# Three graph-attention layers and a relation layer on one core: layer 1's edge weights as a minimum with the mask

## The reference, cut to what matters

```python
def _L1_gnn_ref(x, adj, W, a):
    h = jnp.einsum('bnf,fo->bno', x, W)
    s1 = h @ a1
    s2 = h @ a2
    e = jax.nn.leaky_relu(s1[:, :, None] + s2[:, None, :], negative_slope=0.2)
    att = jnp.where(adj > 0, e, jnp.float32(NEG_BIG))
    att = jax.nn.softmax(att, axis=1)
    h_prime = jnp.einsum('bij,bjo->bio', att, h)
    return jax.nn.elu(h_prime)
...
x = _layernorm(x + _L0_gnn_ref(...))
x = _layernorm(x + _L1_gnn_ref(...))
x = _layernorm(x + _L2_gnn_ref(...))
x = _layernorm(x + _L3_gnn_ref(...))
```

## Time and profile before

| what | before |
|---|---|
| runs | 468.24, 469.8, 472.76 us |
| the profiled execution's own time | 469.28 us |
| its span | 467.5 us |
| TensorE matmul busy | 384.9 us (82%) |
| VectorE busy | 380.4 us (81%) |
| ScalarE busy | 358.4 us (77%) |
| GpSimd busy | 295.8 us (63%) |

### The profile page before, as it was taken

How to read it: one execution, slowest core, us unless ns; L and a number is a source line. 1 busy time by engine, 2 the same in 40 slices (tenths; PEclk the granted TensorE clock), 3 DMA queues, 4 the chain that set the end, 5 groups by cost and what they waited for, 6 DMA issues and landing times. The chain is left out here.

```text
span 467.5 us, 9322 instructions
## 1 busy us (share of the span) xinstructions
PE 384.9 (82%) x2825; PEld 338.0 (72%) x2825; DVE 380.4 (81%) x1384; ACT 358.4 (77%) x869; POOL 295.8 (63%) x425
## 2 busy tenths in 40 slices
PE   2799998999677697796787896999999959989870
PEld 2699997998666586686786796989888856555440
DVE  0358889988978899999999864889889897888862
ACT  1577998999857889899889846578778747787864
POOL 4237886777553463553554665677777776878883
PEclk9999999999888988998898889899999998999985
DMA  6999661000000000000000000000000000011112
GB/s 163 226 248 236 150 103 28 2 1 1 2 1 1 1 1 1 2 0 1 2 1 0 3 1 1 1 2 1 1 2 1 2 1 1 19 65 54 68 72 92
DMA packets 8757, 18.21 MB, mean 39 GB/s; under 512 B 1280, under 2 KB 2560, under 8 KB 8704
## 3 DMA queue, kind: packets, MB, share of 16 engines
q0 software_dynamic: 2304, 8.39, 9.6%
q1 hardware_dynamic: 2976, 4.52, 2.9%
q10 hardware_dynamic: 3424, 4.66, 2.9%
HBM read 21.76 MB, written 4.19 MB: 56 GB/s over the span
## 5 line engine op out<-in xcount | busy, mean ns | idle before, releaser
L459 PE MATMUL o_ps<-h_scaled,PT 128*128 128x129 f32 (+1 forms) x1536 | 191.8, 286 | 12.5 <-DVE y L947 9.6
L459 PEld LDWEIGHTS o_ps<-h_scaled,PT 128*128 128x128 f32 x1536 | 186.9, 202 | 13.7 <-issue 10.1
L676 ACT ACTIVATE X<-y,offset,rstd 128x128 f32<-128x128 f32 x256 | 104.7, 480 | 21.4 <-POOL offset L268 21.3
L897 DVE SCALAR_TENSOR_TENSOR PT<-rows_ps,factors,MT 128x512 f32<-128x512 f32 x128 | 88.9, 736 | 0.0
L401 PE MATMUL h_ps<-wx,xT 128*128 128x130 f32 x384 | 69.1, 322 | 3.9 <-DVE smax L863 2.5
L259 POOL TENSOR_TENSOR rstd<-var_eps,neg_half 128x4 f32<-128x4 f32 x64 | 66.0, 1031 | 5.0
L401 PEld LDWEIGHTS h_ps<-wx,xT 128*128 128x128 f32 x384 | 59.0, 219 | 13.5 <-issue 12.1
L967 DVE BATCH_NORM_STATS2 stats<-y 128x6 f32<-128x128 f32 x256 | 55.9, 280 | 6.6
L649 ACT ACTIVATE edge<-edge,col_tmp,col_full 128x512 f32<-128x512 f32 x64 | 48.4, 803 | 14.9 <-DVE edge L875 14.9
L249 POOL TENSOR_TENSOR h_scaled<-hx,col_tmp 128x512 f32<-128x512 f32 x16 | 16.7, 1042 | 56.2 <-DVE col_tmp L915 56.2
L225 POOL TENSOR_TENSOR mean_term<-h_mean,empty_row 128x512 f32<-128x512 f32 x32 | 38.2, 1193 | 18.4 <-DVE residual L947 16.6
(11 more groups left out here) (99 smaller groups left out, 693.4 us busy)
## 6 DMA issues: line engine op xcount, KB each, us to landing
MT<-adj_by_j POOLq DMA_DIRECT2D x16, 512.0 KB, 10.3
X<-x SPq DMA_DIRECT2D x16, 256.0 KB, 6.1
out<-X ACTq DMA_DIRECT2D x16, 256.0 KB, 2.0
w_rel<-w SPq DMA_DIRECT2D x1, 256.0 KB, 5.6
w_back<-w_by_output ACTq DMA_DIRECT2D x1, 192.0 KB, 3.4
wx<-w_by_input ACTq DMA_DIRECT2D x1, 192.0 KB, 5.4
bias<-b ACTq DMA_DIRECT2D x1, 64.0 KB, 4.8
bias<-b SPq DMA_DIRECT2D x1, 64.0 KB, 9.7
```

What stands on the lines that cost most here:

```text
L459: last = pe.matmul(o_ps[it.b][:, ic, first:1 + D], PT[:, it.b, jc, ic * P:(ic + 1) * P], h_scaled[:, it.b, jc, first:1 + D], start=(jc == ...
L676: last = act.activation(X[:, g, c, :], y[:, b, c, :], ACT.Identity, bias=offset[:, b, c:c + 1], scale=rstd[:, b, c:c + 1])
L897: dve.scalar_tensor_tensor(out=PT[:, it.b, c, :], in0=rows_ps[:], scalar=factors[:, it.b, 1, c:c + 1], in1=m, op0=ALU.max, op1=ALU.mult, * ...
```

## The change: what it does

Layer 1's weight of an edge is exp(leaky(s1 + s2)) divided by a factor that is constant in a column. Before, VectorE formed the exponent, max(s1 + 0.8 s2, 0.2 s1), ScalarE exponentiated it with a bias and a scale per column, and VectorE multiplied the result with the mask. Now ScalarE exponentiates the spread scores themselves, once per item: q = exp(0.2 s) and, in place in PSUM, r = exp(s). VectorE forms max(q x U, r), with U a number per column (`WEIGHT`), and takes the minimum of that with the mask (0, or 1, or `empty_col`), instead of the product. An empty column gets U = 3e38 (`big_col`, made in layer 0 with one small op more per item), so that the minimum gives 1.

For this the scores are shifted by the maximum ahead of being spread (`node_terms`, two small VectorE ops), so that `spread_rows` waits for the shifted scores instead of for `hx`; `column_hinge` is one small ScalarE op, `column_weight` one small VectorE op. The ScalarE slot has its copies of h and of the transpose ahead of the normalisation. The VectorE slot has `own_max(at(3))` right behind the edges, all four `weights` in a row, the maximum of at(3) taken at the slot's end (it was taken at the start of the next), and behind that `add_elu`, statistics and `aggregate` of at(-1). `attend` now waits for `y_sum` in layer 1 too.

```diff
@@ spread_rows, attend (TensorE) @@
-                    pe.wait_ge(sem("hx"), it.done)
+                    pe.wait_ge(sem("below"), it.of_layer)
...
-                if it.done > 2 and item(it.done - 3).l == 0:
+                if it.done > 2 and item(it.done - 3).l < 2:
@@ ScalarE @@
-            def column_exponents(it):
...
+            def column_hinge(it):
+                act.wait_ge(sem("above"), it.of_layer)
+                act.activation(col_tmp[:, it.b, HINGE, :], col_tmp[:, it.b, ABOVE, :], ACT.Exp, scale=SLOPE - 1)\
+                    .then_inc(sem("hinge"), 1)
...
-                act.activation(q_rows[:, :], rows_ps[:], ACT.Copy, scale=SLOPE).then_inc(sem("rows_taken"), 1)
-
-            def edges(it, cs):
-                if cs[0] == 0:
-                    act.wait_ge(sem("col_bias"), it.of_layer)
-                for c in cs:
-                    act.wait_ge(sem("edge_lin"), it.g * C + (c + 1))
-                    act.activation(edge[:, c, :], edge[:, c, :], ACT.Exp, bias=col_tmp[:, it.b, BIAS, c:c + 1],
-                                   scale=col_full[:, it.g, c:c + 1]).then_inc(sem("edge"), 1)
+                act.activation(q_rows[:, :], rows_ps[:], ACT.Exp, scale=SLOPE)
+                act.activation(rows_ps[:], rows_ps[:], ACT.Exp).then_inc(sem("rows_taken"), 1)
@@ VectorE @@
-                    dve.tensor_scalar(col_tmp[:, it.b, R_EIGHTY, :], hx[:, it.r, :, S2], 1 - SLOPE, None,
-                                      ALU.mult).then_inc(sem("r_eighty"), 1)
...
-                dve.wait_ge(sem("exponent"), it.of_layer)
-                dve.scalar_tensor_tensor(out=t[:, BIAS, :], in0=t[:, EXPONENT, :], scalar=shifts[:, it.b, 1:2],
-                                         in1=minus_full[:, it.g, :], op0=ALU.add, op1=ALU.mult)\
-                    .then_inc(sem("col_bias"), 1)
+            def node_terms(it):
+
+                dve.wait_ge(sem("smax"), it.done)
+                if it.g >= 2:
+                    dve.wait_ge(sem("rows_ps"), it.done - 2)
+                dve.tensor_scalar(col_tmp[:, it.b, BELOW, :], hx[:, it.r, :, S1], smax[:, it.b:it.b + 1], LOWEST,
+                                  ALU.subtract, ALU.max).then_inc(sem("below"), 1)
+                dve.tensor_scalar(col_tmp[:, it.b, ABOVE, :], hx[:, it.r, :, S2], smax[:, it.b:it.b + 1], 0.0,
+                                  ALU.add, ALU.max).then_inc(sem("above"), 1)
+
+            def column_weight(it):
+
+                dve.wait_ge(sem("hinge"), it.of_layer)
+                dve.wait_ge(sem("big_col"), it.of_layer)
+                dve.tensor_tensor(col_tmp[:, it.b, WEIGHT, :], col_tmp[:, it.b, HINGE, :], big_col[:, it.g, :],
+                                  ALU.max).then_inc(sem("col_weight"), 1)
+
+            def edges(it):
                 dve.wait_ge(sem("rows_taken"), it.of_layer)
+                dve.wait_ge(sem("col_weight"), it.of_layer)
                 for c in range(C):
-                    dve.scalar_tensor_tensor(out=edge[:, c, :], in0=rows_ps[:], scalar=t[:, R_EIGHTY, c:c + 1],
-                                             in1=q_rows[:, :], op0=ALU.add, op1=ALU.max)\
-                        .then_inc(sem("edge_lin"), 1)
+                    dve.scalar_tensor_tensor(out=edge[:, c, :], in0=q_rows[:, :],
+                                             scalar=col_tmp[:, it.b, WEIGHT, c:c + 1], in1=rows_ps[:],
+                                             op0=ALU.mult, op1=ALU.max).then_inc(sem("edge_lin"), 1)
...
                         dve.scalar_tensor_tensor(out=PT[:, it.b, c, :], in0=m, scalar=empty_col[:, it.g, c:c + 1],
-                                                 in1=edge[:, c, :], op0=ALU.max, op1=ALU.mult,
+                                                 in1=edge[:, c, :], op0=ALU.max, op1=ALU.min,
...
+                dve.tensor_scalar(big_col[:, it.g, :], col_sum[:, it.b, :], 0.0, BIG, ALU.is_equal, ALU.mult)\
+                    .then_inc(sem("big_col"), 1)
```

More of the change, by code:

```diff
@@ L27 @@
 LAST_ATTENTION, ATTENTION_END = G * LAYERS - 4, G * LAYERS + 3
-R_EIGHTY, EXPONENT, BIAS, Z, RZ = range(5)
+R_EIGHTY, EXPONENT, BIAS, Z, RZ, ABOVE, BELOW, HINGE, WEIGHT = range(9)
+LOWEST, BIG = -430.0, 3e38
 class Item:
@@ L1001, in attention_slot @@
                 if at(1) and at(1).l == 1:
-                    column_terms(at(1))
+                    edges(at(1))
+                if at(2) and at(2).l == 1:
+                    node_terms(at(2))
+                if at(3) and at(1) and at(1).l == 1:
+                    own_max(at(3))
                 if at(-2) and at(-2).l == 0:
```

64 lines of the change are left out of this document (27 added, 37 removed).

## The result

The changed kernel takes 473.99 us in the median of 20 runs, the kernel before, run beside it, 470.69 (20 runs): a ratio of 1.0066, 95% interval 1.0047 to 1.0084. So it is slower by 3.3 us, where 466.1 was forecast and 473.0 was the range's upper end. The direction is wrong, and so is the size.

A forecast was written before the change was run, and what follows sets the result against it. VectorE's list was taken to bound the kernel, partly stalled behind GpSimd. Body -5.3, beginning +1.4 and end +0.5 gave -3.4 us on 469.28, 465.9, stated as 466.1; range 461 to 473, the forecast's own 463 to 468.5.

The forecast's parts named there:

- VectorE's list is the bound, and about 0.8 us of each slot is L869 behind GpSimd: Layer 1's body: VectorE busy 93.78 of 95 us, with L869 waiting about 0.8 us per slot for GpSimd's scaling.
- New slot: 8.59 - 0.86 - 0.07 + 0.21 + 0.24 = 8.11 us: Layer 1's body: L869 and the hx op go, three small ops and order costs come; 0.48 us gained per slot.
- The column weight meets no GpSimd op: VectorE in the body: the new op with two SBUF inputs was taken at 0.07 us, at worst 0.93.
- In the third ... 13.3 us: Layer 1's third slot: y, statistics and aggregation behind the maximum, about 2 us in the open, then the flag's round trip.
- The fourth loses its old wait for the late normalisation: 8.3 ... 9.7: Layer 1's fourth slot: 8.3 us with TensorE at the high clock, 9.7 if idle time has lowered it.
- the chain edges, y, attention, maximum is untouched: Layer 1's beginning: this chain stays, with 0.2 us more ahead of y; first two slots 11.2 and 11.1 us.
- ... and 0.1 for the own maximum that now waits for hx: Layer 1's last slot: 0.1 us lost because the own maximum stands ahead of the weights and waits for hx.
- Rival 3: The stall moves: column weight or node terms meet GpSimd as L869 did; slot 8.97, total 475.4 us; chance 0.06.
- ScalarE's slack of 1.0: Layer 1's body: hinge ready at T + 12.7 us, wanted at T + 13.7, so it isn't waited for.
- two passes, 1.1 us or so: Layer 1's beginning: ScalarE makes two passes behind the spread rows, where one of 0.6 us lay beside L869.
- Rival 2: VectorE's wait at the maximum for TensorE replaces the stall; slot 8.4 to 8.6, total 473.0 us; chance 0.14.
- The end, +0.4 behind the last own maximum: Layer 1's end: 2 us of y and statistics against attention 0.5 sooner and perhaps 2.4 shorter; between -0.9 and +1.5.

The follow-up runs named there:

- e1: The kernel before, its arithmetic kept, with only L869 (the column's bias) issued ahead of the reciprocal that releases GpSimd's scaling: 461.44 us, ratio 0.9804.
- e2: The changed kernel with y and its statistics put back between the second and third weights, aggregation still last: 466.16 us, ratio 0.9914.
- e10: e2 with one node term, the one for the hinge, made by ScalarE instead of VectorE: 462.66 us, ratio 0.9817.
- e4: The changed kernel with the maximum of layer 2's first two items also taken at the slot's end, ahead of y: 470.92 us, ratio 1.0016.
- e3: The changed kernel with the node terms of layer 1's first item moved behind the second weight of that slot: 473.38 us, ratio 1.0020.
- e9: The changed kernel with all of VectorE's order undone, ScalarE's copies still ahead of the normalisation: 465.82 us, ratio 0.9899.
- e5: The changed kernel with the old order on both VectorE and ScalarE, new arithmetic kept: 470.23 us, ratio 0.9982.
- e12: e1 with ScalarE's copies of h and of the transpose ahead of the normalisation in layer 1: 462.18 us, ratio 0.9832.

## Why the prediction was wrong

- *VectorE's list is the bound, and about 0.8 us of each slot is L869 behind GpSimd*: right, shown by e1.
- *"New slot: 8.59 - 0.86 - 0.07 + 0.21 + 0.24 = 8.11 us"*: the mechanism was right, with no wait in the body, but three terms were too small. The two node terms take 0.13 each from start to start, not 0.07: that was read from ops without a scalar per partition. The aggregation's gap was put at 0.08 and is 0.19. The sum behind the last weight starts 0.12 later than a further weight would (0.79 for 0.67), where 0.04 was estimated. Sum, column weight and reciprocal took 0.05 less than forecast, and other gaps were a little smaller too. The slot is 8.28, and the body gains 3.3 us instead of 5.3. e2 shows 0.2 of the slot to be y's new place and e10 0.13 one node term.
- *The column weight meets no GpSimd op*: right, 149 to 164 ns in sixteen.
- *"In the third ... 13.3 us"* and *"The fourth loses its old wait for the late normalisation: 8.3 ... 9.7"*: the step that failed. The mechanism had been seen, that the moved y stands in the open behind a maximum that waits for attention. The attention was taken at the 5.45 us that before shows, with 0.69 of the clock granted, and it took 6.76, with 0.54. TensorE's further idle time (2.49 at the flag) was allowed for only in the upper figure for the fourth slot, 9.7, and that too was short: projection 1.94 for 1.13, attention 5.23 for 3.75, and 10.66 in all. The two slots take 25.6 us where the forecast had 22.3 at its middle, and all four 3.5 more than its 44.6. e4's trace shows which part is which: with the third attention at 5.44 the third slot is 13.49 and the fourth 9.53, as forecast, but the long attention stands in the second slot, 12.32 for 11.1, and the four take 1.9 more than the forecast. So the term that failed is "the chain edges, y, attention, maximum is untouched": one attention in it runs 0.9 to 1.3 us longer in every trace of the new arithmetic, and why it does is open. What y's own place costs in the third slot, "about 2 us in the open", was right.
- *"... and 0.1 for the own maximum that now waits for hx"*: 1.7. I had noticed that the own maximum waits in the last slot and not that the projection before it stands behind a maximum which, for the items of layer 2 only, was still taken behind y. e4 shows it, with 1.8 us in that slot.
- *Rival 3, "the column weight, or the node terms, meet GpSimd"*: it happens, at one place, where layer 0's scaling and mean term stand beside item 16's node terms. I had weighed it only for the body, at 0.86 in each slot. e3 gives 0.7 us at the trace, not resolved in the medians.
- *ScalarE's slack of 1.0, "two passes, 1.1 us or so"*: in the body right; at the beginning the edges wait 0.63 us for the second exponential, one part of the 1.3 at the start that I had at none.
- *Rival 2, the maximum's wait in the stall's place*: its price of 473.0 is near the result, its story is only half of it. It needs the wait in all slots, with 8.4 to 8.6 in the body; the trace has it in the first four. What was true of it is "the fourth slot recovers nothing".
- *The end, +0.4 behind the last own maximum*: nothing to be seen; from layer 2's first weights to the own maximum before takes 25.51 us and after 25.43. That "half of the 4.84 goes" at the high clock was too much in any case: this attention ran at 0.77 of the clock, and takes about 3.7 at 1.00.

The sum of the forecast had one good term and three thin ones. (Its 465.9 and the 0.5 to the median make 466.4, not 466.1.) The ends were given 1.9 us and cost 6.6 and 1.3 at the start. What it lacked was to follow the new order through the slots in which TensorE is late already.

And the wider point: e9 and e1 show what the parts are worth. The arithmetic with the copies ahead gives 4.7 us (e9 against its before), the late y and early maxima take 8 away. But moving L869 removes the same stall for 8.9 us and no new small ops, and beyond that stall the runs show no gain from the arithmetic. e5, the new arithmetic in the old order, can't be told from before. e12 has e9's order with the old arithmetic and L869 moved, and is 3.6 us faster than e9 (its executions 460.14 to 463.58, those of e9 464.10 to 468.03).

## What to carry to other kernels

Before work is taken off an engine, look whether the op at the head of the stall can simply be issued at another time; here one moved line did as much as the best version of a new algorithm, and 12.5 us more than the change itself. When an order is changed in a software pipeline, price it in its worst slots and not in its steady ones: an op that is moved behind a wait costs nothing where the wait is short and its whole length where it is long, and the idle time that it gives TensorE can be paid again in the clock. And an engine that is busy only 57% of the time can set the pace: what counts is what stands in its queue behind an op that waits.
